# Eight linear attention layers in four streams: a table of 22 steps per layer in place of 16, and the second batch 5 steps behind the first in place of 8

## What is computed

```python
def _ln(x, g, b):
    m = jnp.mean(x, axis=-1, keepdims=True)
    v = jnp.mean((x - m) ** 2, axis=-1, keepdims=True)
    return (x - m) * jax.lax.rsqrt(v + 1e-05) * g + b

def _phi(t):
    return jax.nn.elu(t) + 1.0

def layer(h, p):                      # 2 sequences of 1024 tokens; D, H, L, F = 128, 16, 8, 512
    q = _phi((h @ wq + bq_).reshape(b, s, H, DH))
    k = _phi((h @ wk + bk_).reshape(b, s, H, DH))
    v = (h @ wv + bv_).reshape(b, s, H, DH)
    kv = jnp.einsum('bshd,bshm->bhdm', k, v)
    z = 1.0 / (jnp.einsum('bshd,bhd->bsh', q, k.sum(axis=1)) + 1e-06)
    att = jnp.einsum('bshd,bhdm,bsh->bshm', q, kv, z).reshape(b, s, d)
    h = h + att @ wo + bo_
    h = _ln(h, g1_, be1_)
    y = jax.nn.gelu(h @ w1 + c1_, approximate=False) @ w2 + c2_
    return (_ln(h + y, g2_, be2_), None)
h, _ = jax.lax.scan(layer, x, params)     # 8 layers, one after the other
return _ln(h, gf, bef)
```

## The kernel before

| step | PE | ACT | DVE | POOL |
|---|---|---|---|---|
| 0 | kv: keys and values | exp, relu | biases, phi(k) | |
| 1 | q | exp, relu | phi(q) | |
| 2 | m: sum over keys | column copy | mask kvm, ks | |
| 3 | num and den | num copy | den: reciprocal, split in three | |
| 4 | turn | rows copy | | |
| 5 | wide | | att | |
| 6 | out | | add (`mid`) | |
| 7, 8, 9 | norm a: turn, -, back | -, -, out | stats, normal, - | root at 7 |
| 10, 11, 12 | up 0 1, up 2 3, down | gelu 0 1, gelu 2 3, - | -, -, add (`end`) | |
| 13, 14, 15 | norm b: turn, -, back | -, -, out | stats, normal, - | root at 13 |

## Time and profile before

### The profile page before, as it was taken

One profiled execution on the slowest core, in us unless ns is written; L12 is line 12 of the kernel. 1 busy time (PEld: TensorE's weight loads), 2 busy tenths in 40 slices (PEclk: granted clock), 3 DMA queues, 4 the chain that ended last, 5 costly groups with the idle time before them and its releaser, 6 DMA issues.

```text
span 4945.9 us, 64634 instructions
## 1 busy us (share of the span) xinstructions
PE 4279.1 (87%) x24264; PEld 2059.2 (42%) x24264; DVE 2961.3 (60%) x6559; ACT 2483.4 (50%) x4251; POOL 1119.3 (23%) x1582
## 2 busy tenths in 40 slices
PE   7888779999888889999886788888888988879989
PEld 4222345655522246555552235444443334333333
DVE  5888456666488846665347965555556653466622
ACT  3588534454358754554445543444433663236642
POOL 1000113333200023332024641111121003420024
PEclk9899887888879978988888998999987999979999
DMA  1100101111010011110000000000001100000000
GB/s 50 24 21 8 44 33 43 33 29 36 34 25 20 9 56 38 33 31 17 11 5 0 0 8 8 16 8 16 8 31 24 24 8 1 28 21 21 14 1 9
DMA packets 48024, 104.19 MB, mean 21 GB/s; under 512 B 15064, under 2 KB 15064, under 8 KB 46432
## 3 DMA queue, kind: packets, MB, share of 16 engines
q1 hardware_dynamic: 47712, 100.06, 7.4%
HBM read 40.24 MB, written 1.05 MB: 8 GB/s over the span
## 4 chain that ended last, share of the span: by engine, by line
PE 57%; DVE 18%; ACT 7%; POOL 2%; issue 2%; SPq 1%; DMA 0%; POOLq 0%; DVEq 0%; ACTq 0%
PE PS L446 29%; PE PS L1029 6%; PE PS L976 4%; DVE SM L1103 4%; DVE AR L2350 3%; PE PS L2532 2%; PE PS L1008 2%; ACT AR L453 2%; DVE AR L450 2%; PE PS L1667 1%; DVE AR L531 1%; PE PS L1712 1%; PE PS L1657 1%; POOL SV L543 1%; ACT PS L2293 1%
## 5 line engine op out<-in xcount | busy, mean ns | idle before, releaser
L1103 DVE TENSOR_REDUCE SM<-PS 128x1 f32<-128x512 f32 (+3 forms) x1792 | 1028.8, 627 | 257.3 <-PE PS L976 159.6
L446 PE MATMUL PS<-AR,WS 128*128 128x512 f32 (+1 forms) x2112 | 1082.7, 651 | 113.3 <-DVE AR L450 32.4
L1077 ACT ACTIVATE AR<-PS 128x1024 f32<-128x1024 f32 (+3 forms) x896 | 825.5, 933 | 339.7 <-PE PS L1011 171.5
L453 ACT ACTIVATE AR<-PS 128x512 f32<-128x512 f32 (+6 forms) x760 | 449.6, 599 | 699.1 <-PE PS L446 425.1
L976 PE MATMUL PS<-AR 51*128 51x512 bf16 (+3 forms) x1792 | 526.6, 390 | 162.0 <-DVE SM L1103 99.2
L446 PEld LDWEIGHTS PS<-AR,WS 128*128 128x128 f32 (+1 forms) x2112 | 395.3, 202 | 561.0 <-issue 371.9
L1735 ACT ACTIVATE AR<-PS,SM 128x128 f32<-128x128 f32 x512 | 229.6, 452 | 467.2 <-DVE SM L1798 464.3
L1029 PE MATMUL PS<-AR 128*32 128x512 f32 (+3 forms) x3584 | 449.7, 575 | 1.3 <-ACT AR L1077 0.9
L976 PEld LDWEIGHTS PS<-AR 51*128 51x128 bf16 x1792 | 129.9, 94 | 679.0 <-DVE SM L1103 477.2
L1008 PE MATMUL PS<-AR 51*128 51x512 bf16 (+3 forms) x1792 | 385.8, 366 | 11.8 <-ACT AR L1077 11.0
L1136 POOL CAST MBT<-SM 128x8 bf16<-128x8 f32 x128 | 28.0, 219 | 1277.5 <-DVE SM L1107 1052.5
(11 more groups left out here) (314 smaller groups left out, 7365.7 us busy)
## 6 DMA issues: line engine op xcount, KB each, us to landing
TP<-RAW SPq DMA_DIRECT2D x512, 64.0 KB, 2.0
AR<-AR SPq DMA_DIRECT2D x768, 32.0 KB
WS<-wall SPq DMA_DIRECT2D x4, 3654.5 KB, 11.1
WS<-wall SPq DMA_DIRECT2D x8, 902.5 KB, 4.6
WS<-wall SPq DMA_DIRECT2D x2, 3334.5 KB, 10.9
WS<-wall SPq DMA_DIRECT2D x1, 2384.0 KB, 9.3
WS<-wall SPq DMA_DIRECT2D x1, 1543.5 KB, 6.1
AR<-pad SPq DMA_DIRECT2D x88, 12.0 KB
```

The lines of the kernel that those rows point to most:

```text
L446: t = e.matmul(o, l, r, start=(n == 0), stop=(n == len(pairs) - 1))
L453: return e.activation(o, i, ACT.Copy, scale=1.0)
L1077: e.activation(pv[:, :, off:512], sv[:, :, off:512], ACT.Exp, scale=scale).then_inc(*F.at_exp.up((s, u, p2)))
L1103: e.tensor_reduce(mh[:, at, k0 // 512:k0 // 512 + 1], bank(ring(n + g), m), AX.X, ALU.max, negate=True).then_inc(*F.at_max.up((s, k, i, rr ...
```

## The change

Every stream's layer gets 22 steps in place of 16, on all four engines alike, and the second batch begins 5 steps behind the first in place of 8. No instruction of arithmetic is added or removed, no wait is added or removed, and no operand, bank or slot is another one.

| step now | PE | ACT | DVE | POOL |
|---|---|---|---|---|
| 0, 1 | kv, q | exp and relu of k, of q | phi(k), phi(q) | |
| 2 | - | - | - | |
| 3, 4, 5, 6 | m, num and den, turn, wide | column, num copy, rows, - | kvm and ks, den, -, att | |
| 7, 8 | -, out | - | -, add | |
| 9 to 13 | norm a: turn, -, -, -, back | out at 13 | stats, normal, -, -, - | root at 9 |
| 14, 15, 16 | up 0, up 1 2, up 3 | gelu 0, gelu 1 2, gelu 3 | - | |
| 17, 18 | -, down | - | -, add | |
| 19, 20, 21 | norm b: turn, -, back | -, -, out | stats, normal, - | root at 19 |

Empty steps: one behind q, one behind wide, two in norm a, one ahead of down. The up-projection is cut in three steps (1, 2 and 1 products per stream) in place of two.

The diff, cut to its core (ACT's and DVE's functions get the same empty steps as PE's):

```diff
@@ -13,7 +13,7 @@
-OFFSET = 8
+OFFSET = 5
@@ -452,7 +452,7 @@
-        def ln_pe(e, w, k, src, ready, chunks, A, B, sq=(0, 1, 2, 3)):
+        def ln_pe(e, w, k, src, ready, chunks, A, B, sq=(0, 1, 2, 3), gap=0):
...
-            yield
-            yield
+            for _ in range(2 + gap):
+                yield
...
@@ -530,10 +530,10 @@
-            yield
-            yield
-
-        def ln_pool(e, w, k, chunks):
+            for _ in range(2 + gap):
+                yield
+
+        def ln_pool(e, w, k, chunks, gap=0):
...
-            yield
-            yield
-            yield
+            for _ in range(3 + gap):
+                yield
@@ -733,9 +735,8 @@
-            yield
-            yield
-            yield
+            for _ in range(4):
+                yield
@@ -847,8 +850,9 @@
                 mm(e, bank(b), (w1[:, ts_(m)], n[:, cs(c)])).then_inc(*F.mlp_up.up((k, c, m)))
                 free[b] = F.mlp_gelu.on((k, c, m))
-                if m % 2:
+                if m != 1:
                     yield
+            yield
@@ -2415,7 +2420,7 @@
-                yield from ln_pe(e, w, (k, "a"), r1, lambda c: [F.la_sum.on((k, c))], chunks, A, B, sq)
+                yield from ln_pe(e, w, (k, "a"), r1, lambda c: [F.la_sum.on((k, c))], chunks, A, B, sq, 2)
@@ -2455,10 +2460,10 @@
-                for _ in range(7):
+                for _ in range(9):
                     yield
-                yield from ln_pool(e, w, (s0 + l, "a"), [c])
-                for _ in range(3):
+                yield from ln_pool(e, w, (s0 + l, "a"), [c], 2)
+                for _ in range(5):
                     yield

```

More of the change, by code:

```diff
@@ L482, in ln_stats, with ln_act @@
             return tiles4(LNS[:, 36 * c:36 * c + 24]), tiles4(LNS[:, 36 * c + 24:36 * c + 32]), SV[:, 4 * c:4 * c + 4]
-        def ln_act(e, w, k, dst, chunks, A, B, g=None, b=None, sq=(0, 1, 2, 3)):
+        def ln_act(e, w, k, dst, chunks, A, B, g=None, b=None, sq=(0, 1, 2, 3), gap=0):
             if len(chunks) == 4:
@@ L497, in ln_act, with ln_dve @@
             yield
-        def ln_dve(e, w, k, chunks, A, sq=(0, 1, 2, 3)):
+        def ln_dve(e, w, k, chunks, A, sq=(0, 1, 2, 3), gap=0):
             def centred(c):
@@ L2430, in layers_act @@
                 yield from la_act(e, w, k, W, chunks, banks, own)
-                yield from ln_act(e, w, (k, "a"), h1, chunks, A, B, W("g1"), W("be1"), sq)
+                yield from ln_act(e, w, (k, "a"), h1, chunks, A, B, W("g1"), W("be1"), sq, 2)
                 yield from narrow_act(e, w, k, W("c1"), c, banks, own)
@@ L2449, in layers_dve @@
                 yield from la_dve(e, w, k, W, chunks, banks, own, mid)
-                yield from ln_dve(e, w, (k, "a"), chunks, A, sq)
+                yield from ln_dve(e, w, (k, "a"), chunks, A, sq, 2)
                 yield from narrow_dve(e, w, k, c, banks, end)
```

## The result

The changed kernel takes 4863.70 us (median of four runs, 4857.12 to 4876.96), the kernel before 4941.59 us beside it: ratio 0.9846, 95% interval 0.9818 to 0.9875. It is faster by 1.5%, 78 us. The forecast was 4877.5, 14 us too high, and the range held: 68.4 us less were forecast and 78 came.

What follows compares the result with a forecast made beforehand. TensorE was nearest the bound, idling in small waits mostly ended by DVE. Work 62.7, waits 10.35 and clock 2.0 gave 75.0 us a layer; eight layers plus ends 622.2 against 690.6, so 4877.5 us, range 4846 to 4916.

Steps and rivals of the forecast that it cites:

- the forecast's 62.7: TensorE's own work in a layer for both batches, 62.7 us at full clock, untouched by the change.
- Step 4's 1.6: TensorE, after norm b's turn back, waits 1.6 us for the second stream's reciprocal parts from DVE.
- Step 7's 1.0: TensorE waits 1.0 us for the first batch's normal, which DVE runs only after the second batch's reciprocals.
- Step 6's 0.3: The second batch's num on TensorE waits 0.3 us for ks.
- The clock's 2.0: One stretch of 4 us at half rate in each layer costs 2.0 us; bounds 0 and 4.1.
- The head: Beginning of the layers: second batch's work missing, but low clock there; -3 us, bounds -9 and 0.
- The tail: Behind the eighth period: first batch's last turn, second batch's down and what followed the last down, 25.2 us.
- the forecast's own: The main case: 74 to 77 us a layer, program 4862 to 4893 us, chance 0.51.
- the rival in which the queue closes up: DVE starts earlier than allowed and the clock stays up: 72 us a layer, 4853 us; chance 0.15.
- step 1's wait: The first q on TensorE waits 0.5 us, behind the bias and ACT's exp load; 1.9 by the skill's rule.
- The rival that the waits come back: Late DVE and ACT handovers add up in steps 4 to 7: 79 us a layer, about 4910 us; chance 0.22.
- the clock stays low through the sparse stretch: Grant stays at 1.2 GHz between 16 and 46 us of a layer: 86 us a layer, 4966 us; chance 0.07.

Runs made afterwards that it cites:

- e7: The changed kernel with an unread product ahead of the wait for the reciprocal's parts, for streams 1 and 3: 4862.70 us, ratio 0.9845.
- e4: The changed kernel with a one-column exp behind the first batch's last gelu, putting two table loads back in each layer: 4865.16 us, ratio 0.9833.
- e12: The changed kernel again, unedited, on another group's chip: 4870.17 us, ratio 0.9854 to the kernel before.
- e2: The changed kernel with the old distance, OFFSET 8 in place of 5: 5076.48 us, ratio 1.026.
- the early phi(k): The changed kernel with the second batch's last phi(k) of a stream moved on DVE to the end of its kv step: 4850.31 us, ratio 0.9811.
- e1: The kernel before with OFFSET 5 in place of 8 and the old 16 steps: 4961.44 us, ratio 1.0036.
- e3: The changed kernel without the two empty steps in norm a, 20 steps in all: 4889.44 us, ratio 0.9883.

## Why the prediction was right

**The period** was to be 75.0 us and is 72.4, the clock's cost included. With e7's 71.20 at full clock, 1.2 us of it is clock. If TensorE's own work is the forecast's 62.7, 8.5 us are waits with their drains; before, these were 15.2, and about 4.1 of clock, which is an estimate from the mean grant. So of the 9.6 us that a layer gained, about 6.7 are waits and 2.9 the clock.

The 62.7 is itself a little too large: in e7, at full clock, the second half takes 26.1 us from the second batch's out to the next kv, without a wait, and the forecast's terms for it sum to 26.9. Counting e7's waits as the forecast did, from the end of the issued work and with the fillers inside them, gives about 9.2 us where 10.35 was forecast, and 62.0 for the work. The 2.6 us that the period was too long are thus about 1.2 of waits, 0.7 of own work and 0.8 of clock.

**The order of the walk** held in all its steps. From the first batch's kv on, forecast and measured start: norm b's turn 12.8 and 12.8, m 14.4 and 14.3, the second batch's kv 23.6 and 23.4, its m 32.3 and 32.3, its num 36.45 and 36.2, the down-projection 55.6 and 55.5 (3219.77 less 3164.24). The waits, counted in that way from e7's timeline:

| step and wait | forecast, us | e7, us |
|---|---|---|
| 1, q | 0.5 | 0.6 |
| 2, norm b's turn | 0.5 | 0.5 |
| 3, num for ks | 1.0 | 1.05 |
| 4, the second stream's parts | 1.6 | 1.1 |
| 5, m for phi(k) | 1.3 | 1.1 |
| 6, norm a's turns | 1.2 | 1.2 |
| 6, num for ks | 0.3 | 0 |
| 7, the parts | 2.3 | 2.0 |
| 7, ACT's rows | 0.5 | 0.5 |
| 7, the normal | 1.0 | 0.7 |
| 7, att and out | 0.15 | 0.1 |
| not forecast, around wide | 0 | 0.3 |

**The mis-sized terms:**

- Step 4's 1.6 for the parts is 1.1: DVE is done with them at 23.0 (3187.01 + 0.23) in place of 23.3, and TensorE comes to them a little later.
- Step 7's 1.0 for the normal doesn't show in the changed kernel. DVE starts the first batch's normal at 41.8 in place of 42.5. The turns back of its two streams, from 43.5, run at the low clock and take 1.94 us together, in which the second stream's normal ends. At full clock, in e7, the wait is there with 0.49 us, 0.7 with its drain. So the trace of the changed kernel has a part of this wait as clock.
- Step 6's 0.3 for ks is nothing: DVE does the mask and the column (3199.61 and 3200.13 us) while TensorE is in the norm's turn, and num follows at 3200.42.
- The clock's 2.0 are 1.2 (72.4 less 71.20). The stretch was right: the only one is around the first batch's turn back of norm a, from 43 to 47 us into the layer, and to 50 in the two longer layers.
- The head, -3 us, is +1.9: the first layer takes 74.28 us against 72.4. Num and den wait 2.96 us there for ks and run partly at the low clock, as the earlier trace rows had shown, and the second batch's missing work doesn't make up for it. The tail, forecast as 25.2, is 25.3 if the eighth layer is taken as 72.1 us long (3623.69 - 3526.26 - 72.1).

In sum: 8 x 1.85 for waits and own work and 8 x 0.8 for the clock less 4.9 for the head is 16.3, and the stage is 622.2 - 606.0 = 16.2 us shorter than forecast.

**Which case it was.** By the mechanism, the forecast's own. By the period, 72.4, it is the rival in which the queue closes up (72 us), which had 0.15; the median, 4863.7, lies within the forecast's own 4862 to 4893 only by its edge, 11 us above what that rival gave. Even this edge is generous: the forecast's own layers were 74 to 77 us, and by its sum 74 us gives 4869.5; 4862 belongs to 73.1 us.

The rule of the 1.38 us of drain beside each table load (the Trainium skill, "ScalarE: Activation LUTs", section "What ACT_TABLE_LOAD costs") would have made step 1's wait 1.9; it is 0.50, or 0.6 with the drain of the products, so the trace doesn't agree. The rival that the waits come back isn't borne out: the waits in steps 4 to 7 sum to 4.6 us in the timeline above, and to 7.0 at full clock with drains in e7, where 8.35 was forecast. That the clock stays low through the sparse stretch didn't come about here, but was no idle fear: at distances of 4 and 8 the clock is 0.86 and 0.84.

**Where luck helped.** The layers gained 84.6 us and the program's median shows 78 of them. With all of them the median would be 4857, outside the forecast's own. And two errors pulled apart: the periods were 21 us too long in sum, the head 4.9 us too short.

**What isn't settled:** why the fifth and the sixth layer of the changed kernel (73.5 and 72.6 us, clock 0.95) have more of the lower clock than the others, from the same queue. It isn't chance: e4 and e12 have the same two layers, with the same lengths within 0.02 us. With fillers the sixth is longer as well, 72.7 us. Nor did a run take out the empty steps behind q, behind wide or ahead of down, so what each of them is worth isn't shown.

## What to carry to other kernels

When several chains share in-order engines, walk one period on every engine, ACT too, before moving the chains against each other: the walk of the change did so and came within 3 us of a layer of 72. The expectation for e2 named two waits, was off by 22, and had neither the gelus between the exps nor the clock. A table of steps and its distance are one parameter; try the neighbours of the distance, but don't expect a slope. Where waits are left on TensorE, ask first whether they pull its clock down: in this stage a product that nobody reads, put in the wait, was cheaper than the low clock, and with it the early phi(k) gained twice as much (15.1 us of stage in place of 7.7).

## What was not expected of the hardware

Equal idle time on TensorE had different prices. The kernel before and e1 are idle for 13 us a layer alike, at a clock of 0.95 and of 0.86 to 0.90, and the layer takes 82.0 and 85.4 us. In e3 the clock's part of the loss (2.2 us of busy time) is four times that of the wait (0.5). And the reverse: 1.77 us of added products raised the clock from 0.98 to 1.00 and took 0.8 us off the shown layer and 0.9 off the mean.
